# Feature attention of a decoder's third layer: per-token head products on VectorE and GpSimd, or head rounds on rotated rows with sums on TensorE

## Chip, cores and metric
The kernel runs on one core of a Trainium2 chip. The metric is the device time of one execution in microseconds (us), the median of three runs. The core has five engines with queues of their own: TensorE (PE; its weight loads are shown as PEld), VectorE (DVE), ScalarE (ACT), GpSimd (POOL) and SyncE (SP), which here issues transfers (DMA).

## The reference, cut to the stage that changes
The program is a four-layer decoder in float32 over 4 sequences of 256 tokens with 256 features: twelve stages (attention, cross attention or state space, feed forward, per layer), each of the form x = x + f(layernorm(x)). The change lies in the seventh, the third layer's attention. It has 16 query heads and 8 key and value heads of 16 features each; key head h // 2 serves query head h.

```python
q = rope(h @ Wq.T + bq); k = rope(h @ Wk.T + bk); v = h @ Wv.T + bv      # per head, 16 features
def feats(x, R):
    x = x / max(sqrt(sum(x * x)), 1e-6)
    p = einsum('...d,ed->...e', x, R)                                    # R is 8 x 16
    return concatenate([sin(p), cos(p)], -1) / sqrt(16)
qp, kp = feats(q, R), feats(repeat(k, 2), R)                             # b h s f
kv  = einsum('bhsf,bhsd->bsfd', kp, repeat(v, 2))                        # summed over the heads h
out = einsum('bhsf,bsfd->bhsd', qp, kv)
out = out.reshape(b, s, 256)          # heads before tokens, not transposed back
return out @ Wo.T + bo
```

There is no sum over tokens: for each token the output of query head h is the sum over the 8 key heads k of (qp[h] . kp[k]) * v[k], times 2. The `reshape` mixes heads and tokens, so the result has to be stored by heads and read back as rows.

## The kernel before
T = 1024 tokens, P = 128 partitions, KD = 2 chunks of 128 features, TILES = 8 tiles of 128 tokens, HALF = 512. PSUM is used as four "pairs" of 1024 float32 columns (`m.pair(0)` to `m.pair(3)`). `Jobs` hands the pairs out in turn: a named job is filled by PE and emptied by the engine named with it, and a job waits until the one four places before it has been emptied. Stages follow one another through the residual `m.resid`; the next stage begins when this one's last addition to it is done.

`feature_attention` runs in this order:
- The layer norm (`norm_vector`, `norm_gpsimd`, `norm_tensor`, `norm_scalar`) leaves the turned rows in `m.hT`, features on partitions.
- PE projects q0, q1 and k0 with features on partitions (`project`, L239), each twice, the second time with the halves of a head exchanged; DVE rotates them (`rotate`, L1556 and L1559) and squares them (L2229). Then PE makes v with tokens on partitions (L2173), and DVE adds its bias (L2231).
- PE sums the squares of each head (L2182); ACT takes the root (L2207), DVE inverts it. PE multiplies by the random matrix (L2189), which also puts tokens on partitions; DVE scales and reduces the angles (L2247 to L2252); ACT takes the sine (L2211).
- The body: for each of 8 tiles of 128 tokens `head_products` makes all 8 x 8 x 16 products of a query chunk with the keys, a reduction sums over the 16 features (L2267), a second `head_products` multiplies weights with values, and a reduction sums over the 8 key heads (L2259). The products of query chunk 0 are made on DVE, those of chunk 1 on GpSimd; all reductions are DVE's. PE does nothing here. SP stores each finished tile by heads to `l2a_scratch` (L2139).
- The end: SP loads the four sequences back as rows (L2143); PE turns them (L2196), ACT copies them to `m.hT` (L2215), PE projects with Wo (`project_tokens`, L252), DVE adds the bias (L261) and the result (L267).

A float32 matmul is two PE instructions in the trace's counts; a PE transpose is one.

Of the kernel before, what the change touches and what calls it, by code (L numbers as in the profile page):

```python
# [20 lines left out]
ALU = mybir.AluOpType  # L21
# [2067 lines left out]
def feature_attention(m, n, j):  # L2089

    nc = m.nc
    tag = "l2a_"
    w = lambda name: m.w[tag + name]
    HPC, HD = 8, 16
    chunks = [("q", 0), ("q", 1), ("k", 0)]
    jobs = Jobs(m, tag + "in", 2, [(f"{x}{c}{s}", "vector") for x, c in chunks for s in ("", "s")]
                + [("v", "vector"), ("norm", "scalar")] + [(f"p{x}{c}", "vector") for x, c in chunks]
                + [("t0", "scalar"), ("t1", "scalar"), ("out0", "vector"), ("out1", "vector")])  # L2100
    tmp = [m.sb(tag + f"rot{i}", [P, B, S]) for i in range(2)]
    x = {f"{k}{c}": m.sb(tag + f"{k}{c}", [P, T]) for k, c in chunks}
    sq = {f"{k}{c}": m.sb(tag + f"sq_{k}{c}", [P, T]) for k, c in chunks}
    feats = {"q0": m.pair(1), "q1": sq["q1"][:], "k0": sq["k0"][:]}
    v = m.sb(tag + "v", [P, TILES, P])
# [4 lines left out]
    weight = [m.pair(3)[:, 0:HPC * HPC].rearrange("p (k q) -> p k q", q=HPC), m.sb(tag + "weight1", [P, HPC, HPC])[:]]  # L2110
    att = m.sb(tag + "att", [P, TILES, D])
    (rotated, turns_ready, feats_ready, v_ready, pair_done, weight_done, value_done, att_done) = (
        m.sem(tag + s) for s in ("rotated", "turns", "feats", "v_ready", "pair", "weight", "value", "att"))

    def head_products(eng, ops, c, t, step, done):


        if step == 0:
            q = feats[f"q{c}"][:, t * P:(t + 1) * P].rearrange("p (h f) -> p h f", f=HD)
            k = feats["k0"][:, t * P:(t + 1) * P].rearrange("p (h f) -> p h f", f=HD)  # L2120
            ops.tensor_tensor(pair_prod[c][:], q.unsqueeze(1).to_broadcast([P, HPC, HPC, HD]),
                              k.unsqueeze(2).to_broadcast([P, HPC, HPC, HD]), ALU.mult).then_inc(done, 1)
        else:
            g = weight[c].rearrange("p k q -> p q k").unsqueeze(2).to_broadcast([P, HPC, HD, HPC])
            vt = v[:, t, :].rearrange("p (k d) -> p d k", d=HD).unsqueeze(1).to_broadcast([P, HPC, HD, HPC])
            ops.tensor_tensor(value_prod[c][:], g, vt, ALU.mult).then_inc(done, 1)
# [5 lines left out]
    with nc.Block(name=tag + "block", no_gpsimd_drain=True) as block:  # L2132
# [13 lines left out]
        def _(pool):  # L2146
# [5 lines left out]
            for t in range(TILES):  # L2152
# [4 lines left out]
                if t:  # L2157
                    pool.wait_ge(att_done, 2 * t)
# [847 lines left out]
```

## Time and profile before

| | |
|---|---|
| median of 3 runs | 1628.77 us (1625.76 to 1629.52) |
| time of the profiled execution | 1629.11 us |
| its span, first to last instruction | 1627.3 us |
| mean granted TensorE clock | 0.843 of full |
| the stage (first norm instruction to last addition) | 870.63 to 1011.33 us |
| of it the body (products and reductions) | 925.3 to 989.1 us |
| of it the end (store, load, turn, project, add) | 989.1 to 1011.3 us |

The span is 1.8 us shorter than the execution's own time; the difference lies outside the instructions. "PEclk" in the rows is the clock granted to TensorE: 1.00 is 2.4 GHz and 0.50 is 1.2 GHz. In the views by window, the columns are the window, its length, the busy time and number of instructions of each engine, the granted clock, the mean busy share of the 16 DMA engines, and what they moved.

### The profile page before, as it was taken

How to read it: one execution, taken by the hardware profiler on the slowest of the kernel's cores; microseconds unless marked ns; L12 is line 12 of the kernel's file. 1: busy time of each engine (PE TensorE's matmuls, PEld its weight loads, DVE VectorE, ACT ScalarE, POOL GpSimd, SP SyncE). 2: the span in 40 equal slices, each digit the busy share in tenths (PEclk: the TensorE clock that was granted, in tenths of full speed). 3: DMA queues.
4: the chain of work that ended last, by engine and by line, in shares of the span. 5: the costliest groups of instructions: out<-in, count | busy, mean ns of one | idle time of the engine just before them, and what ended most of it. 6: DMA issues, size and time to landing. Idle time of an engine off the chain costs nothing. (4 is left out here: it accounts for less than half of the span.)

```text
span 1627.3 us, 20923 instructions
## 1 busy us (share of the span) xinstructions
PE 1088.7 (67%) x5866; PEld 694.1 (43%) x5866; DVE 1082.2 (67%) x1807; ACT 486.5 (30%) x943; POOL 600.8 (37%) x604
## 2 busy tenths in 40 slices
PE   7545548999218795555998503699847878866970
PEld 3211135776015672113565402577534324445860
DVE  6999975873686548998885795320345868845454
ACT  3423322333402342332221100333313346632430
POOL 0046614552754115661000272023431632214746
PEclk9669977999559897997998756899878969986995
DMA  5064347995321404435100011142520040038944
GB/s 188 30 258 150 108 156 225 313 309 207 98 61 46 112 3 156 154 104 208 41 1 0 0 16 36 47 140 81 164 87 10 26 131 3 3 116 238 340 143 121
DMA packets 135201, 188.51 MB, mean 116 GB/s; under 512 B 34736, under 2 KB 98242, under 8 KB 133836
## 3 DMA queue, kind: packets, MB, share of 16 engines
q1 hardware_dynamic: 100956, 138.51, 26.9%
q0 software_dynamic: 12704, 29.36, 6.2%
q10 hardware_dynamic: 21456, 19.60, 3.8%
q8 instruction: 42, 0.69, 0.2%
q14 instruction: 43, 0.35, 0.1%
HBM read 142.80 MB, written 31.72 MB: 107 GB/s over the span
## 5 line engine op out<-in xcount | busy, mean ns | idle before, releaser
L165 POOL TENSOR_SCALAR rstd<-moments 128x4 f32<-128x4 f32 x24 | 6.5, 269 | 406.0 <-DVE moments L148 406.0
L177 PE MATMUL psum<-w_ident,h 128*128 128x128 f32 x144 | 29.6, 388 | 112.1 <-DVE h L155 112.1
L558 PE MATMUL psum<-l0s_read,w_ident 128*128 128x512 f32 x128 | 65.2, 634 | 52.6 <-DVE l0s_read L623 52.6
L558 PE MATMUL psum<-l1s_read,w_ident 128*128 128x512 f32 x128 | 65.3, 636 | 52.3 <-DVE l1s_read L623 52.3
L1906 DVE TENSOR_REDUCE l3x_neg<-psum 128x2 f32<-128x512 f32 x128 | 80.7, 684 | 23.2 <-PE psum L1777 23.2
L546 POOL TENSOR_TENSOR l1s_drive<-l1s_du,l1s_bc 128x1024 f32<-128x1024 f32 x32 | 75.3, 2353 | 35.3 <-DVE psum L619 35.3
L546 POOL TENSOR_TENSOR l0s_drive<-l0s_du,l0s_bc 128x1024 f32<-128x1024 f32 x32 | 75.3, 2353 | 35.3 <-DVE psum L619 35.3
L1881 ACT ACTIVATE l3x_work<-psum 128x512 f32<-128x512 f32 x128 | 72.7, 599 | 50.9 <-PE psum L1800 50.6
L1028 POOL DMA_INDIRECT l0f_x<-l0f_h_rows,l0f_token_now x56 | 60.4, 1078 | 50.3 <-PE psum L1152 23.7
L1162 PE MATMUL psum<-l0f_w_in,l0f_xT 128*128 (+1 forms) x224 | 77.9, 472 | 0.1
L1037 POOL DMA_INDIRECT l3f_x<-l3f_h_rows,l3f_token_of x64 | 59.3, 926 | 49.1 <-DVE l3f_token_of L1433 28.6
L177 PEld LDWEIGHTS psum<-w_ident,h 128*128 128x128 f32 x144 | 25.3, 201 | 118.5 <-DVE h L155 116.2
L619 DVE TENSOR_TENSOR_SCAN psum<-psum,l0s_drive 128x1024 f32<-128x1024 f32 x32 | 73.2, 2286 | 0.0
L619 DVE TENSOR_TENSOR_SCAN psum<-psum,l1s_drive 128x1024 f32<-128x1024 f32 x32 | 73.2, 2286 | 0.0
L189 ACT ACTIVATE hT<-psum 128x512 f32<-128x512 f32 x36 | 19.4, 596 | 163.8 <-PE psum L177 163.7
L558 PEld LDWEIGHTS psum<-l0s_read,w_ident 128*128 128x128 f32 x128 | 22.4, 195 | 95.3 <-DVE l0s_read L623 79.5
L558 PEld LDWEIGHTS psum<-l1s_read,w_ident 128*128 128x128 f32 x128 | 22.4, 195 | 95.2 <-DVE l1s_read L623 79.2
L595 ACT ACTIVATE psum<-late,w_l1s_a 128x1024 f32<-128x1024 f32 x32 | 35.7, 1118 | 80.0 <-DVE l1s_read L623 79.4
L595 ACT ACTIVATE psum<-l0s_delta,w_l0s_a 128x1024 f32<-128x1024 f32 x32 | 35.7, 1117 | 80.0 <-DVE l0s_read L623 79.4
L1181 PE MATMUL psum<-l0f_w_down,l0f_gatedT 88*128 (+1 forms) x224 | 57.6, 380 | 0.0
L1192 PE MATMUL psum<-l3f_xT,l3f_w_in 128*96 128x96 f32 x528 | 57.0, 252 | 0.5 <-ACT l3f_xT L1293 0.5
L2196 PE MATMUL psum<-w_ident,h 128*128 128x128 f32 x16 | 3.7, 425 | 79.3 <-DMA h<-l2a_scratch 79.3
(635 smaller groups left out, 3145.5 us busy)
## 6 DMA issues: line engine op xcount, KB each, us to landing
l0f_w_in<-in_l0f_w_in SPq DMA_DIRECT2D x56, 352.0 KB
l0s_bc<-l0s_scratch SPq DMA_DIRECT2D x16, 1024.0 KB, 5.2
l1s_bc<-l1s_scratch SPq DMA_DIRECT2D x16, 1024.0 KB, 5.1
l3f_w_in<-in_l3f_w_in SPq DMA_DIRECT2D x32, 384.0 KB
l0f_w_down<-in_l0f_w_down SPq DMA_DIRECT2D x56, 176.0 KB
l2f_w_in<-in_l2f_w_in SPq DMA_DIRECT2D x24, 352.0 KB
l0f_y_rows<-l0f_y ACTq DMA_DIRECT2D x56, 128.0 KB
l3f_w_down<-in_l3f_w_down SPq DMA_DIRECT2D x32, 192.0 KB
```

Of the source, the lines that this page charges most:

```text
L177: ins = nc.tensor.transpose(m.psum[:, at:at + P], m.h[:, t, k * P:(k + 1) * P], m.ident[:])
L546: nc.gpsimd.tensor_tensor(drive[c], du[:, c, :], bc[s][:, 0, :], ALU.mult).then_inc(drive_ready, 1)
L558: ins = nc.tensor.matmul(m.pair(2 + c)[:, cols], lhsT=m.ident[:], rhs=rhs[:, cols], start=start, stop=stop, skip_group_check=True)
L595: nc.scalar.activation(decay[c], delta[:, c, :], ACT.Exp, scale=w["a"][:, c, bass.ds(at, 1)]).then_inc(decay_ready, 1)
L619: nc.vector.tensor_tensor_scan(state[c], decay[c], drive[c], 0.0, ALU.mult, ALU.add).then_inc(scanned, 1)
L1028: nc.gpsimd.indirect_dma_start(x[s][:], None, h_rows, bass.IndirectOffsetOnAxis(ap=token_now[s // 2][:, s % 2:s % 2 + 1], axis=0)).then_in ...
L1037: nc.gpsimd.indirect_dma_start(x[b % ROWS][0:L, :], None, h_rows, bass.IndirectOffsetOnAxis(ap=token_of[0:L, b:b + 1], axis=0)).then_inc(x ...
L1162: ins = nc.tensor.matmul(in_ps[d % 2], lhsT=xT[d % 2][:, k, :], rhs=w, start=(k == 0), stop=(k == KD - 1))
L1181: ins = nc.tensor.matmul(y_ps[d % 2], lhsT=gatedT[d % 2][:, c, :], rhs=w, start=(c == 0), stop=(c == chunks - 1))
L1192: ins = nc.tensor.matmul(feature_ps[i][:, f, :], lhsT=w_in[:, at, k, f * F:(f + 1) * F], rhs=xT[i][:, k, 0:L], start=(k == 0), stop=(k == ...
L1881: nc.scalar.activation(self.prob[i % 8][:, 0:self.keys], self.bank(3 + i % 3)[:, 0:self.keys], ACT.Exp).then_inc(self.exp_done, 1)
L1906: ins = nc.vector.tensor_reduce(self.neg[k % 2][:, :, hl], bank[:, 0:self.keys].rearrange("p (q k) -> p q k", q=self.maxima), AX_X, ALU.ma ...
```

## The change
The body is written anew, and what stands around it follows.
- **Layout.** v is projected with features on partitions too. After the sine, PE turns the features of k0, q0 and q1 back (eight transposes each, new jobs `fk0`, `fq0`, `fq1`), and ACT copies them to rows: the keys to `keys[:, 0, :]`, the queries to `q_rows`. The order of the chunks is now k0, q0, q1. ACT, no longer DVE, adds v's bias, into `values[:, 0, :]`.
- **Rotated copies.** SP makes seven copies of the values and seven of the keys, rotated by 16 r partitions (one head), SBUF to SBUF: two transfers a copy. Values: 14 transfers of 1024 columns. Keys: 14 for each half of the tokens, 28 in all, of 512 columns.
- **Rounds.** For each half of the tokens and each rotation r (16 steps) DVE multiplies both query chunks with the rotated keys (`by_heads`, 1024 elements a partition), PE multiplies by a 128 x 128 matrix of ones within a head, so each feature row holds the head pair's weight (`weigh`, two 512-column matmuls), DVE multiplies that from PSUM with the rotated values (`mix`), and PE adds the product to a running sum in PSUM with the identity (`add`, two 512-column matmuls). PE's order is weigh(s), add(s - 1).
- **Sums.** For each half ACT copies the sums, PE turns them in eight transposes (`turn_sums`; the first half's stand in PE's order at step 10), ACT copies them to `att`, SP stores four tiles and loads two sequences, PE turns eight blocks (`turn_rows`), ACT copies (`take_rows`), PE projects (`project_out`), DVE adds. The bias of the output is added to the residual before the norms' wait, not at the end. GpSimd has only its part of the layer norm.

```diff
+    chunks = [("k", 0), ("q", 0), ("q", 1)]
+    keys, values = (m.sb(tag + s, [P, ROUNDS, T]) for s in ("keys", "values"))
+    turned_to = {"k0": keys[:, 0, :], "q0": q_rows[:, 0, :], "q1": q_rows[:, 1, :]}
+    weights_ps = [m.pair(2 + i).rearrange("p (c t) -> p c t", c=KD) for i in range(2)]
-    pair_prod = [m.sb(tag + f"pair_prod{c}", [P, HPC, HPC, HD]) for c in range(KD)]
-    value_prod = [m.sb(tag + f"value_prod{c}", [P, HPC, HD, HPC]) for c in range(KD)]
+    prod = [m.sb(tag + f"prod{i}", [P, KD, HALF]) for i in range(2)]
+    mixed = [m.sb(tag + f"mixed{i}", [P, KD, HALF]) for i in range(3)]
+    def rotate_heads(sp, rows, r, cols, sem):
+        at = P - HD * r
+        sp.dma_start(rows[0:at, r, cols], rows[HD * r:P, 0, cols]).then_inc(sem, 16)
+        sp.dma_start(rows[at:P, r, cols], rows[0:HD * r, 0, cols]).then_inc(sem, 16)
...
         def _(sp):
+            sp.wait_ge(jobs.empty("v"), 1)
+            for r in range(1, ROUNDS):
+                rotate_heads(sp, values, r, slice(0, T), values_in)
+            sp.wait_ge(jobs.empty("fk0"), 3)
+            for h in range(2):
+                for r in range(1, ROUNDS):
+                    if h:
+                        sp.wait_ge(keys_in[r], 32)
+                    rotate_heads(sp, keys, r, halves[h], keys_in[r])
+            for h in range(2):
+                sp.wait_ge(att_done, h + 1)
+                for t in range(4 * h, 4 * h + 4):
+                    dst = scratch[t // 2, :, t % 2 * P:(t % 2 + 1) * P, :].rearrange("h s d -> s h d")
+                    sp.dma_start(dst, att[:, t, :].rearrange("p (h d) -> p h d", d=HD)).then_inc(stored[t // 2], 16)
+                for b in range(2 * h, 2 * h + 2):
+                    sp.wait_ge(stored[b], 32)
+                    sp.dma_start(m.h[:, 2 * b:2 * b + 2, :], rows[b]).then_inc(att_back[h], 16)
...
         def _(pool):
             norm_gpsimd(m, pool, n)
-            head_products(pool, nc.gpsimd, 1, 0, 0, pool_pair)
-            for t in range(TILES):
...
...
         def _(pe):
-            jobs.wait_room(pe, "v")
-            for t in range(TILES):
-                for k in range(KD):
...
+            project(m, pe, jobs, "v", wcols(w("v"), 0), hT, KD)
+            def weigh(s):
+                pe.wait_ge(prod_done, s + 1)
+                if s >= 2:
+                    pe.wait_ge(mix_done, s - 1)
+                for c in range(KD):
+                    ins = nc.tensor.matmul(weights_ps[s % 2][:, c, :], lhsT=w("same")[:], rhs=prod[s % 2][:, c, :], start=True,
+                                           stop=True)
+            def add(s):
+                h, r = divmod(s, ROUNDS)
+                pe.wait_ge(mix_done, s + 1)
+                for c in range(KD):
+                    ins = nc.tensor.matmul(m.pair(h)[:, c * HALF:(c + 1) * HALF], lhsT=m.ident[:], rhs=mixed[s % 3][:, c, :],
+                                           start=(r == 0), stop=(r == ROUNDS - 1), skip_group_check=True)
+            for s in range(STEPS):
+                weigh(s)
+                if s:
+                    add(s - 1)
+                if s == ROUNDS + 2:
+                    turn_sums(0)
+            add(STEPS - 1)
+            turn_rows(0)
+            turn_sums(1)
+            project_out(0)
+            turn_rows(1)
+            project_out(1)
...
         def _(act):
+            nc.scalar.activation(values[:, 0, :], jobs.pair("v"), ACT.Identity, bias=w("v_b")[:, 0:1])
             for i, (k, c) in enumerate(chunks):
                 act.wait_ge(turns_ready, i + 1)
+                nc.scalar.activation(sq[f"{k}{c}"][:], sq[f"{k}{c}"][:], ACT.Sin, scale=SIN_SCALE).then_inc(feats_ready, 1)
+                jobs.wait_filled(act, f"f{k}{c}")
+                nc.scalar.activation(turned_to[f"{k}{c}"], jobs.pair(f"f{k}{c}"), ACT.Copy)
+            take_sums(0)
+            take_sums(1)
+            take_rows(0)
+            take_rows(1)
...
         def _(dve):
+            o.link(dve, nc.vector.tensor_tensor(m.resid[:], m.resid[:], w("o_b")[:].unsqueeze(1).to_broadcast([P, TILES, D]),
+                                                ALU.add))
+            dve.wait_ge(jobs.empty("norm"), 2)
...
-            for t in range(TILES):
-                head_products(dve, nc.vector, 0, t, 0, pair_done)
...
-            add_tokens(m, dve, jobs, ("out0", "out1"), bias=w("o_b")[:])
+            def by_heads(s):
+                if r:
+                    dve.wait_ge(keys_in[r], 32 * (h + 1))
+                nc.vector.tensor_tensor(prod[s % 2][:], q_rows[:, :, halves[h]],
+                                        keys[:, r, halves[h]].unsqueeze(1).to_broadcast([P, KD, HALF]), ALU.mult).then_inc(prod_done, 1)
+            def mix(s):
+                dve.wait_ge(weighed, s + 1)
+                if s == 1:
+                    dve.wait_ge(values_in, 32 * (ROUNDS - 1))
+                nc.vector.tensor_tensor(mixed[s % 3][:], weights_ps[s % 2],
+                                        values[:, r, halves[h]].unsqueeze(1).to_broadcast([P, KD, HALF]), ALU.mult).then_inc(mix_done, 1)
+            by_heads(0)
+            for s in range(STEPS):
+                if s + 1 < STEPS:
+                    by_heads(s + 1)
+                mix(s)
```

## Rows read from the trace of the kernel before
**Rows 1.** The page: busy time of each engine over the span.
```profile
span 1627.3 us, 20923 instructions
PE 1088.7 (67%) x5866; PEld 694.1 (43%) x5866; DVE 1082.2 (67%) x1807; ACT 486.5 (30%) x943; POOL 600.8 (37%) x604
```
**Rows 2.** Windows of the stage: before the body, and the body.
```profile
890.00:925.00 35.00, 26.61 (x150) 21.40 (x148) 22.83 (x24) 4.52 (x5) 0.00 (x0) 0.83 0.00 0
925.00:989.00 64.00, 0.00 (x0) 0.00 (x0) 61.11 (x49) 0.23 (x1) 49.81 (x16) 0.50 0.13 14
```
**Rows 3.** Timeline: start, duration, engine, line, operation, idle time before and releaser.
```profile
922.92 1.23 DVE L2252 TENSOR_TENSOR l2a_sq_k<-l2a_sq_k,l2a_whole 128x1024 f32<-128x1024 f32 x1
924.17 1.06 ACT L2211 ACTIVATE l2a_sq_k<-l2a_sq_k 128x1024 f32<-128x1024 f32 x1 [2.65 <-DVE l2a_sq_k L2252]
...
925.33 1.23 DVE L2121 TENSOR_TENSOR l2a_pair_prod<-psum,l2a_sq_k 128x1024 f32<-128x1024 f32 x1 [1.19 <-ACT l2a_sq_k L2211]
...
987.85 1.22 DVE L2259 TENSOR_REDUCE l2a_att<-l2a_value_prod 128x128 f32<-128x1024 f32 x1 [1.05 <-POOL l2a_value_prod L2126]
...
995.89 3.67 PE L2196 MATMUL psum<-w_ident,h 128*128 128x128 f32 x16 [79.29 <-DMA h<-l2a_scratch]
...
1000.68 9.38 PE L252 MATMUL psum<-w_l2a_o,hT 128*128 128x256 f32 x32 [1.11 <-ACT hT L2215]
1006.72 1.23 DVE L267 SCALAR_TENSOR_TENSOR resid<-psum,resid 128x1024 f32<-128x1024 f32 x1 [15.45 <-PE psum L252]
1010.10 1.23 DVE L267 SCALAR_TENSOR_TENSOR resid<-psum,resid 128x1024 f32<-128x1024 f32 x1 [2.15 <-PE psum L252]
```
**Rows 4.** Groups by line and form, from the stage (busy, mean ns; idle and releaser).
```profile
L239 PE MATMUL psum<-hT,w_l2a_k 128*128 128x512 f32 x16 | 7.0, 593 | 0.0
L2173 PE MATMUL psum<-w_l2a_v,hT 128*128 128x128 f32 x32 | 3.7, 275 | 0.0
L2247 DVE TENSOR_TENSOR l2a_sq_q<-psum,l2a_norm 128x1024 f32<-128x1024 f32 x2 | 2.5, 1225 | 1.4 <-PE psum L2189 1.4
L2215 ACT ACTIVATE hT<-psum 128x1024 f32<-128x1024 f32 x2 | 2.0, 1024 | 73.4 <-PE psum L2196 73.4
L2621 PE MATMUL psum<-w_ident,l1f_inner 128*128 128x128 f32 x8 | 1.1, 280 | 1.9 <-DVE l1f_inner L2466 1.9
```
**Rows 5.** Windows that show the granted clock and what PE did.
```profile
820.00:840.00 20.00, 20.00 (x69) 11.67 (x69) 17.09 (x20) 3.07 (x3) 0.00 (x0) 1.00 0.00 1
913.00:916.60 3.60, 3.60 (x32) 3.42 (x31) 3.45 (x4) 0.00 (x0) 0.00 (x0) 1.00 0.00 0
919.50:920.00 0.50, 0.00 (x0) 0.00 (x0) 0.50 (x1) 0.00 (x0) 0.00 (x0) 0.84 0.00 0
1000.50:1005.00 4.50, 4.32 (x10) 3.51 (x11) 0.00 (x0) 0.13 (x1) 0.00 (x0) 0.50 0.00 0
1005.00:1005.50 0.50, 0.50 (x3) 0.39 (x3) 0.00 (x0) 0.00 (x0) 0.00 (x0) 0.83 0.00 0
```
**Rows 6.** Transfers by tile: issue time min/median/max, starts; time to landing min/median/max.
```profile
L2139 SPq DMA_DIRECT2D l2a_scratch<-l2a_att x8: 359/360/389, 937.7 to 989.1; - x8
DMA to landing us min/median/max: 2.9/3.0/3.0
...
L2143 SPq DMA_DIRECT2D h<-l2a_scratch x4: 360/469/940, 989.5 to 992.2; - x4
DMA to landing us min/median/max: 3.2/3.5/4.0
...
L1694 SPq DMA_DIRECT2D l1a_q_packed<-l1a_parts x36: 532/599/767, 496.5 to 552.6; - x36
```
**Rows 7.** Windows: one 128 KB store of the body; SBUF-to-SBUF copies of the second layer.
```profile
938.50:939.00 0.50, 0.00 (x0) 0.00 (x0) 0.50 (x1) 0.00 (x0) 0.50 (x2) 0.50 0.65 67
939.00:939.50 0.50, 0.00 (x0) 0.00 (x0) 0.47 (x2) 0.00 (x0) 0.50 (x1) 0.50 0.92 112
939.50:940.00 0.50, 0.00 (x0) 0.00 (x0) 0.50 (x1) 0.00 (x0) 0.50 (x1) 0.50 0.74 83
...
505.00:510.00 5.00, 5.00 (x13) 2.21 (x12) 3.32 (x3) 0.53 (x1) 1.79 (x1) 1.00 0.26 67
```

More of the change, by code:

```diff
@@ L2111, in feature_attention @@
+    summed = m.sb(tag + "summed", [P, KD, HALF])
     att = m.sb(tag + "att", [P, TILES, D])
[L2112 to L2126, printed above, removed]
@@ new lines, in add, with turn_sums @@
+            def add(s):
[4 more added lines that the diff above has]
+                                           start=(r == 0), stop=(r == ROUNDS - 1), skip_group_check=True)
+                ins.then_inc(added, 1)
+            def turn_sums(h):
+                pe.wait_ge(sums_taken, h + 1)
+                for t in range(4):
+                    for c in range(KD):
+                        ins = nc.tensor.transpose(m.pair(h)[:, t * D + c * P:t * D + (c + 1) * P], summed[:, c, t * P:(t + 1) * P],
+                                                  m.ident[:])
+                ins.then_inc(sums_turned, 1)
@@ new lines, in turn_rows, with project_out @@
+            def turn_rows(h):
+                pe.wait_ge(att_done, h + 1)
+                pe.wait_ge(att_back[h], 32)
+                for c in range(KD):
+                    for t in range(4):
+                        ins = nc.tensor.transpose(m.pair(h)[:, c * HALF + t * P:c * HALF + (t + 1) * P],
+                                                  m.h[:, 4 * h + t, c * P:(c + 1) * P], m.ident[:])
+                ins.then_inc(rows_turned, 1)
+            def project_out(h):
+                pe.wait_ge(hT_done, h + 1)
+                for t in range(4):
+                    for k in range(KD):
+                        ins = nc.tensor.matmul(m.pair(2 + h)[:, t * D:(t + 1) * D], lhsT=m.hT[:, k, (4 * h + t) * P:(4 * h + t + 1) * P],
+                                               rhs=w("o")[:, k, :], start=(k == 0), stop=(k == KD - 1))
+                ins.then_inc(out_filled, 1)
@@ L2205, in _ @@
             norm_scalar(m, act, j)
+            m.wait_weights(act, tag)
+            jobs.wait_filled(act, "v")
+            nc.scalar.activation(values[:, 0, :], jobs.pair("v"), ACT.Identity, bias=w("v_b")[:, 0:1]).then_inc(jobs.empty("v"), 1)
             jobs.wait_filled(act, "norm")
@@ L2279, in context_mixing @@
+            by_heads(0)
[3 more added lines that the diff above has]
+                mix(s)
+            for h in range(2):
+                dve.wait_ge(out_filled, h + 1)
+                r = m.resid[:, 4 * h:4 * h + 4, :]
+                nc.vector.tensor_tensor(r, m.pair(2 + h).rearrange("p (t d) -> p t d", d=D), r, ALU.add).then_inc(out_added, 1)
+            dve.wait_ge(out_added, 2)
 def context_mixing(m, n, j):
@@ L2946, in layouts @@
     d["l2a_v"] = rows_to_chunks(i["L2_attn_Wv"].T)
-    d["l2a_v_b"] = across(i["L2_attn_bv"])
+    d["l2a_v_b"] = column(i["L2_attn_bv"])
     d["l2a_o"] = rows_to_chunks(i["L2_attn_Wo"].T)
```

113 lines of the change are left out of this document (45 added, 68 removed).

## The prediction
> **What bounds the kernel now.** The page comes first: over the span PE and DVE are busy alike, 67% each, so the average names no engine [rows 1]. Then the windows of the stage: in the body DVE is busy 61.1 of 64 us, GpSimd 49.8, and PE not at all, at a granted clock of 0.50; transfers take 13% [rows 2]. So the body is DVE's. The timeline gives its ends: the first product starts at 925.33, the last reduction ends at 989.07, 63.7 us [rows 3]. The stage's end, from there to the last addition at 1011.33, is 22.3 us, and it is a chain with nothing beside it: store, load, 16 transposes from 995.89, copies, 16 matmuls from 1000.68, two additions [rows 3]. The next stage needs the last of them, so a microsecond taken from or put on this chain is one of the kernel's time.
>
> **Before the body.** PE sets this stretch (busy 26.6 of its 35 us, without a gap until the last random product) [rows 2]. v as four 512-column float32 matmuls costs 4 x 0.86 = 3.44 us, from the k0 projection (eight such matmuls, 7.0 us: 0.87 with its edge, 0.43 us an instruction), where it cost 3.7 [rows 4]. I take 0.3 us off all that follows. v's bias on ACT and the output bias (2.3 us of DVE) fall into waits: ACT has nothing to do there, and DVE waits for the norms. Without that cover they would cost 1.0 and 2.3 us.
>
> The last angles are ready at 924.15 in the kernel before [rows 3], so at 923.85. ACT then needs a sine (1.06 us, [rows 3]), PE eight transposes, ACT a copy of 1024 columns (1.02, [rows 4]). Transposes: 16 took 3.67 us at clock 0.50, so 1.84 for eight [rows 3]; at the start of another burst eight took 1.1 us [rows 4]. I take 1.84 for q0's and q1's: the clock fell to 0.50 within 919.5 to 920.0, some 3 us after PE's last work at 916.6 [rows 5]. The three chains queue on ACT: k0's copy ends by about 920.4, q0's at 924.35, q1's at 928.35. The first product starts there instead of at 925.33: **+3.0 us**.
>
> **The sixteen steps.** For DVE a step is two operations of 1024 elements, one of them reading PSUM: 2 x 1.225 = 2.45 us [rows 4]. For PE it is four 512-column matmuls: 4 x 0.86 = 3.44 us at full clock. PE is the longer. Do the waits hold it up? mix(s) needs weigh(s); PE meanwhile does add(s - 1) and weigh(s + 1), 3.44 us, before it needs mix(s), which takes 1.2. by_heads runs a step ahead. So no. The sum: 16 x 3.44 = 55.0 us; the first product before PE can begin, 1.2; the first half's eight transposes inside the steps, 1.1. To this comes the clock. In the end of the kernel before, matmuls started at 1000.68 at clock 0.50 and got full clock in the window from 1005.0 to 1005.5 (mean 0.83) [rows 5], so about 4.4 us at half speed, which loses 2.2. Once up it stays: a stretch of 20 us with PE always busy shows 1.00 [rows 5]. Together 59.5 us: the steps end at 928.35 + 59.5 = 987.9, where the old body ended at 989.07: **-4.2 us** against its 63.7. Bounds: no half-clock start, -2.2; 0.05 us more at each of the 32 handovers (the gap from ACT's last copy to the matmuls at 1000.68 is about that), +1.6.
>
> So 111 us of DVE and POOL work (61.1 and 49.8) become 55 of PE, and the gain is small because DVE and POOL had worked side by side.
>
> **The transfers that must come first.** Values: 7 copies x 128 rows x 4 KB = 3.67 MB from 903.4, after ACT's v; then keys, 7 x 0.26 MB for the first half, from 920.4. SP issues an SBUF-to-SBUF copy in 0.6 us [rows 6]: 14 take 8.4 us. The nearest rate is that of the second layer's SBUF-to-SBUF copies: 67 GB/s at a DMA share of 0.26, 258 GB/s at full share [rows 7]. The values then take 14.2 us, to 918.6, and keys round 1 lands some 3 us after 920.4; it is needed at about 931.8, since weigh(0) ends at 933.0. Later rounds come each 1.2 us and are used each 3.44. Hidden, cost 0. SP has issued everything by 937, long before the first half's stores, and that half's store and load (at about 963 to 975) lie under the steps.
>
> **The end.** From the end of the steps: copy 1.02, eight transposes 1.1 (turn_rows(0) ran during the copy), copy 1.02, with handovers 3.35 us. Then four stores at once. One store occupies all DMA engines for (0.65 + 0.92 + 0.74) x 0.5 = 1.15 us [rows 7] and lands after 3.0 [rows 6], so about 1.85 of latency. Four: 4 x 1.15 + 1.85 = 6.4 us. The second load waits for them and lands 3.2 later (3.2 to 4.0, [rows 6]): 9.6. Then eight transposes 1.84, copy 1.03, eight matmuls 6.0 (the old first half: 1000.68 to its addition at 1006.72, [rows 3]), an addition 1.23, handovers 0.2. The clock is low again, since project_out(0) is over 5 us before. Sum 3.35 + 9.6 + 10.3 = 23.25 against 22.3: **+1.0 us**. Half the turning and projecting has gone under the waits (with project_out(0) as cover); the turning of the sums and three more stores in a burst take it back. Bounds: stores that do not queue, -2.3; matmuls at full clock, -2.6; each store only after the one before has landed (4 x 3.0) and a load of 4.0, +6.4.
>
> **Sum.** +3.0 - 4.2 + 1.0 = -0.2 us. The profiled execution took 1629.11, 0.3 above the median of 1628.77; on it this gives 1628.9, on the median **1628.6 us**. A measurement of this kernel can tell about 0.2%, 3.3 us, from no change.
>
> **Rivals.**
> *A, the clock stays up (faster).* If the transposes before the steps, and those after the load, keep or bring the clock, then the steps lose no 2.2, q1's and the last rows' transposes cost 1.1 (-1.5), the last matmuls 3.4 instead of 6.0 (-2.6): -6.3, 1622.3 us. For it: the clock was still 1.00 for 3 us after PE stopped. Against: in the old end 3.67 us of transposes and 4.5 of matmuls went by at 0.50 [rows 3, 5]. 0.17.
>
> *B, the rotated copies are late (slower).* The slowest rate in the rows is the store's, 131 KB in 1.15 us, 114 GB/s, with runs of 64 bytes [rows 7]. At it, values and keys round 1 (3.93 MB) need 34.5 us from 904.4 and land at 939.7, 7.9 us after 931.8: 1636.5 us. It costs something below 148 GB/s, and more than 0.2% below 131. Against: the copied runs are of 2 and 4 KB. 0.11. The Trainium skill (DMA: Bandwidth & Descriptors, section Bandwidth) says to batch transfers to 1 MiB and more, and gives 138 GB/s for one of 64 KB; by an estimate from that page 3.93 MB take 28.5 us and the kernel is 1.9 us slower, at 1630.5. No row here shows that for transfers queued behind one another.
>
> *C, the last burst (slower).* Four stores and two loads one after another by their landings, as bounded above: +6.4, 1635.0 us. For it: nothing hides them now. Against: stores and loads did overlap before, four loads landing within 6.4 us of the first's issue [rows 3, 6]. It leaves 0.2% from 3.5 us on. 0.13.
>
> *D, PE at half clock through the steps.* 64 x 0.86 more, less the 2.2 counted: +52.8, 1681.4. Rows of long busy stretches speak against it. 0.03.
>
> **Chances.** The forecast has 0.56: of it 0.48 within 0.2%, 0.03 faster, 0.05 slower. With A 0.20 faster; with B, C and D 0.32 slower; 0.48 same. The range runs from A to B, 1622.3 to 1636.5, and leaves out D and the tails. The forecast's own range is 1625 to 1632.
>
> **What the profile of the changed kernel would show.** Steps: PE busy without gaps, a 512-column instruction each 0.43 us, granted clock 1.00 from the second step on, DVE busy some 70%; DVE's waits ended by PE. If mix or by_heads waits for a DMA at step 1, it is B. The first by_heads at 928.4, the last add at 987.9, four stores issued from 991.3, the last transposes from 1000.9, the last addition ending at 1011.1. A last-matmul window at 1.00 shows A; transposes after 1004, C. The prediction is wrong outright if PE's steps take other than 3.44 us.

## The result, and the profile after

| | before | after |
|---|---|---|
| median of 20 runs each | 1627.01 us (1622.46 to 1632.67) | 1633.10 us (1624.84 to 1636.79) |
| ratio to before, 95% interval | | 1.0032 (1.0021 to 1.0042) |
| profiled execution: time, span | 1629.11, 1627.3 us | 1632.82, 1631.0 us |
| mean granted TensorE clock | 0.843 | 0.867 |
| the stage, first norm instruction to the next stage's | 141.52 us | 141.01 us |

By the ratio the changed kernel is slower by 0.32%, 5.2 us (3.4 to 6.8); the two medians are 6.1 us apart, the two profiled executions 3.7. In these two profiles the stage that was changed is not longer. Its parts first: the page, the windows from the last projections to the end of the steps (891.20 to 932.20, then 932.20 to 991.20, with 940 to 985 out of their middle), and the end.

```profile
span 1631.0 us, 21259 instructions
PE 1150.4 (71%) x6010; PEld 720.5 (44%) x6010; DVE 1057.6 (65%) x1790; ACT 494.3 (30%) x951; POOL 550.3 (34%) x588
```
```profile
891.20:932.20 41.00, 33.12 (x156) 23.78 (x154) 26.44 (x26) 10.25 (x10) 0.00 (x0) 0.85 0.46 125
932.20:991.20 59.00, 57.62 (x138) 26.06 (x139) 37.71 (x32) 2.05 (x2) 0.00 (x0) 0.96 0.28 57
940.00:985.00 45.00, 45.00 (x112) 20.37 (x111) 30.68 (x27) 2.05 (x2) 0.00 (x0) 1.00 0.25 38
991.20:1015.00 23.80, 13.11 (x56) 10.23 (x54) 2.45 (x2) 3.98 (x4) 0.00 (x0) 0.78 0.36 44
```
The body was DVE's [rows 2] and is now PE's: 45.00 us busy of 45. DVE has become the one that waits, as the groups of the steps show (busy, mean ns, then idle and releaser): 19.1 us for the sums of `weigh`.
```profile
L2198 PE MATMUL psum<-l2a_prod,w_l2a_same 128*128 128x512 f32 x64 | 31.5, 620 | 2.5 <-DVE l2a_prod L2323 2.5
L2206 PE MATMUL psum<-l2a_mixed,w_ident 128*128 128x512 f32 x64 | 29.9, 592 | 0.0
L2333 DVE TENSOR_TENSOR l2a_mixed<-psum,l2a_values 128x1024 f32<-128x1024 f32 x16 | 19.6, 1224 | 19.1 <-PE psum L2198 19.1
```
The timeline of the changed kernel, with the points that answer to [rows 3]:
```profile
907.52 0.60 SPq L2129 DMA_DIRECT2D l2a_values<-l2a_values  x1
...
923.84 0.51 SPq L2129 DMA_DIRECT2D l2a_keys<-l2a_keys  x1
...
932.21 2.36 DVE L2323 TENSOR_TENSOR l2a_prod<-l2a_q_rows,l2a_keys 128x1024 f32<-128x1024 f32 x2 [4.34 <-ACT l2a_q_rows L2263]
...
933.58 5.23 PE L2198 MATMUL psum<-l2a_prod,w_l2a_same 128*128 128x512 f32 x8 [2.53 <-DVE l2a_prod L2323]
...
987.60 3.60 PE L2206 MATMUL psum<-l2a_mixed,w_ident 128*128 128x512 f32 x8
...
994.49 4.12 SPq L2150 DMA_DIRECT2D l2a_scratch<-l2a_att  x4
...
999.43 3.30 SPq L2153 DMA_DIRECT2D h<-l2a_scratch  x2
1005.16 1.94 PE L2223 MATMUL psum<-w_ident,h 128*128 128x128 f32 x8 [6.01 <-DMA h<-l2a_scratch]
1007.14 1.02 ACT L2274 ACTIVATE hT<-psum 128x1024 f32<-128x1024 f32 x1 [11.77 <-PE psum L2223]
1008.22 5.49 PE L2231 MATMUL psum<-w_l2a_o,hT 128*128 128x256 f32 x16 [1.11 <-ACT hT L2274]
1013.74 1.22 DVE L2345 TENSOR_TENSOR resid<-psum,resid 128x1024 f32<-128x1024 f32 x1 [13.33 <-PE psum L2231]
1016.00 0.43 DVE L145 BATCH_NORM_STATS2 stats<-resid 128x6 f32<-128x256 f32 x1 [1.03 <-PEq L2925]
```
Read against the stage's own start (874.99; 870.63 before): the first product comes at 57.22 us instead of 54.70 (+2.5), the steps last 59.0 instead of 63.74 (-4.7), and from there to the last addition's end it is 23.8 instead of 22.3 (+1.5). Together -0.7, and -0.5 at the next stage's first instruction.

So the time came from elsewhere. Cut at the first norm instruction of each stage (the DVE rows of L145), the profiles of three executions of either program say where:

| stage, us | before: shown, r1, r4 | after: shown, r2, r3 |
|---|---|---|
| third layer's attention (changed) | 141.5, 140.7, 140.7 | 141.0, 143.4, 140.8 |
| the three stages after it, summed | 251.4, 248.0, 248.1 | 247.9, 251.3, 250.5 |
| last attention (l3x) | 185.1, 184.3, 184.1 | 185.4, 186.4, 186.2 |
| last stage, routed experts (l3f), to the end | 178.65, 178.61, 178.57 | 181.62, 181.67, 181.58 |

The three stages summed have a spread of their own (one of them, the third layer's experts, takes 174 or 176 us in either program); so have the stages ahead of the change (experts of the first layer 254.2 to 257.3). The last attention goes with that spread: it is about 1 us longer where the third layer's experts took 176 us. Like compared with like it is 1.2 us longer in the changed kernel: 185.4 against 184.3 and 184.1 beside 174 us, 186.4 and 186.2 against 185.1 beside 176. The changed stage has a spread too: r2's 143.4 us differ from the 141.0 shown above mostly by slower matmuls at the start of the steps (6.62 us for the first eight instructions of `weigh` against 5.23) and in the last projection (6.18 us against 5.49). The last stage has no such spread: +3.0 us, and its instructions are the same. Its start in both kernels, PE and the first norm instruction:
```profile
1448.65 1.40 DVE L145 BATCH_NORM_STATS2 stats<-resid 128x6 f32<-128x256 f32 x4 [0.84 <-PEq L2853]
1452.29 3.63 PE L177 MATMUL psum<-w_ident,h 128*128 128x128 f32 x16 [5.74 <-DVE h L155]
1455.75 3.68 PE L1090 MATMUL psum<-w_l3f_router,hT 128*128 128x64 f32 x32
```
```profile
1449.38 1.41 DVE L145 BATCH_NORM_STATS2 stats<-resid 128x6 f32<-128x256 f32 x4 [1.14 <-PEq L2925]
1453.02 3.68 PE L177 MATMUL psum<-w_ident,h 128*128 128x128 f32 x16 [6.04 <-DVE h L155]
1456.49 6.93 PE L1090 MATMUL psum<-w_l3f_router,hT 128*128 128x64 f32 x32
```
The router's 32 matmuls take 6.93 us instead of 3.68. The windows say why: the last column but two is the granted clock, 0.99 over the router's matmuls before and 0.50 after, 1.2 instead of 2.4 GHz. The first two rows of each block are windows of 2 us from the stage's start on.
```profile
1448.65:1450.65 2.00, 0.00 (x0) 0.00 (x0) 2.00 (x10) 0.00 (x0) 0.22 (x1) 0.56 0.28 51
1450.65:1452.65 2.00, 0.36 (x2) 0.33 (x3) 2.00 (x11) 0.00 (x0) 1.62 (x4) 0.50 1.08 363
1455.65:1460.65 5.00, 3.78 (x34) 3.64 (x32) 1.78 (x11) 1.08 (x2) 0.00 (x0) 0.99 1.08 276
```
```profile
1449.38:1451.38 2.00, 0.00 (x0) 0.00 (x0) 2.00 (x10) 0.00 (x0) 0.22 (x1) 1.00 0.39 73
1451.38:1453.38 2.00, 0.36 (x2) 0.33 (x3) 2.00 (x10) 0.00 (x0) 1.62 (x4) 0.69 0.91 276
1456.38:1461.38 5.00, 5.00 (x26) 5.00 (x24) 0.63 (x6) 1.09 (x2) 0.00 (x0) 0.50 1.09 294
```
At the stage's start the order is the other way round (0.56 and 0.50 before, 1.00 and 0.69 after): in the kernel before the clock fell earlier in PE's pause and was back over the router's matmuls, in the changed one it fell later and stayed down through them.

### The profile page after: what moved, and what is told of

It reads as the page before. It is cut to its first block and busy times, and to the rows that moved or that the text cites. A ratio compares the mean times of both kernels' runs of the same rounds, so it can differ in the third digit from the quotient of the medians.

```text
span 1631.0 us, 21259 instructions
## 1 busy us (share of the span) xinstructions
PE 1150.4 (71%) x6010; PEld 720.5 (44%) x6010; DVE 1057.6 (65%) x1790; ACT 494.3 (30%) x951; POOL 550.3 (34%) x588
## 5 line engine op out<-in xcount | busy, mean ns | idle before, releaser
L177 PE MATMUL psum<-w_ident,h 128*128 128x128 f32 x144 | 29.7, 388 | 112.4 <-DVE h L155 112.4
L1906 DVE TENSOR_REDUCE l3x_neg<-psum 128x2 f32<-128x512 f32 x128 | 80.6, 683 | 23.1 <-PE psum L1777 23.1
L558 PEld LDWEIGHTS psum<-l0s_read,w_ident 128*128 128x128 f32 x128 | 22.3, 194 | 95.5 <-DVE l0s_read L623 79.6
L1777 PE MATMUL psum<-l3x_k_packed,l3x_q_packed 64*128 64x256 bf16 x256 | 43.9, 307 | 12.8 <-ACTq L2031 8.7
```

The source lines that it names most:

```text
L177: ins = nc.tensor.transpose(m.psum[:, at:at + P], m.h[:, t, k * P:(k + 1) * P], m.ident[:])
L558: ins = nc.tensor.matmul(m.pair(2 + c)[:, cols], lhsT=m.ident[:], rhs=rhs[:, cols], start=start, stop=stop, skip_group_check=True)
L1906: ins = nc.vector.tensor_reduce(self.neg[k % 2][:, :, hl], bank[:, 0:self.keys].rearrange("p (q k) -> p q k", q=self.maxima), AX_X, ALU.ma ...
```

## The experiments

Each ratio is to the kernel before on the same chip, with its 95% interval. Increments ("pads") are of semaphores that nothing waits for, put where the engine idles; they change no result. In the compiled kernel before, PE's stream holds 10930 instructions, ACT's 1620, DVE's 2433, GpSimd's 1058, SP's 1005; in the changed one 11236, 1629, 2436, 1034, 1047. All code behind the stage is therefore moved. "Position" below means where in its engine's stream an instruction stands.

**r1, r2: both programs again.** No edit.

> The kernel before once more, unchanged, as the measure of spread. All theories: ratio 1.000 within its interval. In its profile the attention stage (first norm statistic to the next stage's) takes 141.5 us as in the first profile. If the stages that load expert weights differ by 2 to 3 us from the first profile of the same program, then the 3.0 us by which the first expert stage was longer in the changed kernel's profile (254.2 against 257.3 us) is spread between executions and no effect of the change.

> The changed kernel once more, unchanged. Theory 1 (the loss lies inside the stage, in most executions): the stage takes 145 us or more in this profile, against 141.0 in the first. Theory 2 (the loss lies outside the stage, in stages whose instructions are the same): the stage again takes 141 us, the ratio is again 1.002 to 1.004, and the stages before it are some 3 to 5 us longer than in the kernel before. Theory 3 (spread alone): ratio within 0.1% of 1.

Measured 0.9990 (0.9970 to 1.0009) and 1.0031 (1.0011 to 1.0052). The loss repeats. The first experts stage takes 256.6 us in r1 and 255.5 in r2, so its 3 us between the two profiles shown are spread. The stages ahead of the change are not longer in r2 than in r1 (865.6 and 866.1 us together), and the changed stage took 143.4 us, not the 141 expected.

**r3, r4: the inputs' sizes.** The change also alters two small inputs (`v_b`, `ones`/`same`). r3 gives the changed kernel the old sizes, r4 the old kernel the new ones.

```diff
# r3, on the changed kernel: the old sizes; the ones-within-a-head matrix stands in v_b's place, v's bias in that of ones
-rhs=w("same")[:, 0:P:HD] ... lhsT=w("same")[:] ... bias=w("v_b")[:, 0:1]
+rhs=w("v_b")[:, 0:P:HD] ... lhsT=w("v_b")[:] ... bias=w("ones")[:, 0:1]
-("l2a_v_b", [P, 1]) ... ("l2a_same", [P, P])
+("l2a_v_b", [P, P]) ... ("l2a_ones", [P, 8])
# r4, on the kernel before: inputs in DRAM of the new sizes
+                if name == "l2a_v_b":
+                    src = src.partition_broadcast(P)
+                elif name == "l2a_ones":
+                    src = src[:, 0:8]
```

> The changed kernel with the two small inputs of the stage kept at the sizes of the kernel before (64 KB and 4 KB instead of 512 bytes and 64 KB: the ones matrix travels in the place of the value bias and the other way round), so that every input lies in memory as before. If the difference comes from where the inputs lie in memory (a form of theory 2), the ratio falls from 1.003 to 1.000 within 0.1%. If it comes from the stage (theory 1) or from anything else in the new code, it stays at 1.003.

> The kernel before with the two small inputs at the changed kernel's sizes (512 bytes and 64 KB), its code otherwise the same; the bias is spread over the partitions by its transfer. Placement theory: ratio 1.003. Theory 1 and any theory of the new code: 1.000 within 0.1%.

r4: 0.9987 (0.9970 to 1.0004): new inputs don't slow the old kernel. r3: 1.0016 (0.9997 to 1.0035), by itself undecided; its last two stages are the changed kernel's (186.2, 181.6 us). So it is not the inputs.

**r5, r6, r7: the old kernel with the new stream lengths.**

```diff
# r7; r5 has only PE's, r6 all but PE's
+            for _ in range(306):
+                pe.sem_inc(idle[0], 1)       # before pe.wait_ge(att_back, 16 * B)
+            for _ in range(9): act.sem_inc(idle[1], 1)
+            for _ in range(3): dve.sem_inc(idle[2], 1)
+            for _ in range(42): sp.sem_inc(idle[3], 1)
+            for _ in range(232): pool.sem_inc(idle[4], 1)
```

> The kernel before, computing the same; only PE's instruction stream is made 306 instructions longer in the attention stage, by increments of an unused semaphore while PE waits for the loaded rows, so that all later PE code stands where the changed kernel has it. Position theory (the loss comes from where later code stands, and with it the moments at which PE's clock falls and rises): the last attention takes about 185.5 to 186.4 us instead of 184.1 to 185.1, the last expert stage 181.6 instead of 178.6, the ratio is 1.002 to 1.004; if PE's position is what counts. Any theory in which the new work itself carries the loss: both stages as in the kernel before, ratio 1.000.

> The same with the other four streams made longer instead (ACT 9, DVE 3, SP 42, POOL 232 instructions, while they idle; POOL's code is 24 shorter in the changed kernel, and 232 is 256 less 24), PE's left alone. Position theory with another engine's stream: 181.6 us in the last stage here and 178.6 with PE's. New-work theory: nothing moves.

> The kernel before with all five streams made longer. Position theory, whatever the engine: last attention 185.4 or more, last expert stage 181.6, ratio 1.002 to 1.004. New-work theory: 184.5 and 178.6, ratio 1.000.

r5 1.0017 (1.0002 to 1.0033), r6 1.0018 (1.0001 to 1.0035), r7 1.0032 (1.0013 to 1.0051). r7 computes the stage in the old way, takes 141.65 us for it, and loses what the changed kernel loses; its last two stages are 186.2 and 181.2 us. In r5 and r6 the last stage is 178.4 and 178.8 and the router is at 3.7 us: neither PE's stream alone nor the other four alone brings that loss, though either raises the time a little. The router's row of r7 is the changed kernel's:
```profile
1454.10 3.67 PE L177 MATMUL psum<-w_ident,h 128*128 128x128 f32 x16 [6.03 <-DVE h L155]
1457.56 6.93 PE L1090 MATMUL psum<-w_l3f_router,hT 128*128 128x64 f32 x32
```

**r8, r9, r10: other positions.** r8 lengthens GpSimd's stream of the changed kernel to the old length; r9 puts all five streams of the changed kernel where the old ones stood, modulo 256 instructions; r10 adds 256 to four streams of the old kernel (without DVE).

```diff
# r8, on the changed kernel, after GpSimd's norm
+            for _ in range(24): pool.sem_inc(idle[0], 1)
# r9, on the changed kernel: PE 208 (40 before each q chunk's transposes, 40 before the steps, 88 before turn_rows(1)),
#     ACT 247, DVE 253 (before the last addition), SP 214, GpSimd 24
# r10, on the kernel before, at r7's places: PE, ACT, SP, GpSimd 256 each
```

> The changed kernel with 24 increments of an unused semaphore added to POOL, which has nothing to do there, so that POOL's later code stands where the kernel before has it. If POOL's position counts: last expert stage 178.6 us and ratio 1.001; otherwise 181.6 and 1.003 as in the changed kernel.

> The changed kernel, computing the same, with increments of unused semaphores put where the engines idle (PE 208, ACT 247, DVE 253, SP 214, POOL 24), so that every stream's later code is longer than in the kernel before by 512, 256, 256, 256 and 0 instructions. If what counts is the position within blocks of 256 instructions: last expert stage 178.6 us, last attention 184 to 185, ratio 1.000 within 0.1% (the attention stage itself as before or up to 1 us longer, where the increments do not all fit into idle time). If position counts in another way, any ratio from 1.000 to 1.005. New-work theory: 181.6 and 1.003 again.

> The kernel before with 256 increments each on PE, ACT, SP and POOL in idle time. Position within blocks of 256: nothing moves, last expert stage 178.6 us, ratio 1.000. Absolute position, or idle-time increments costing by themselves: ratio 1.002 to 1.003, as with the other padded kernels.

r8 1.0049 (1.0034 to 1.0063), last stage 181.4: GpSimd's position alone takes nothing back, and the time is above either figure expected. r10 0.9994 (0.9974 to 1.0013), last stage 178.5: length alone costs nothing. r9 1.0113 (1.0084 to 1.0141): the later stages came back near the old values (184.4 and 180.0, the router at 3.7 us), but the pads overran the pauses they were put in, and the stage took 157.8 us.

**r11, r12: fewer sums on PE.** The steps are bound by PE, and GpSimd is free. In r11 GpSimd adds the products of two rounds, and PE sums half as often. r12 is r11 with its code brought to the old positions (PE 14, ACT 247, DVE 254, SP 214, GpSimd 10).

```diff
+            for q in range(ROUNDS):
+                pool.wait_ge(mix_done, 2 * q + 2)
+                if q >= 2:
+                    pool.wait_ge(added, q - 1)
+                nc.gpsimd.tensor_tensor(paired[q % 2], mixed[2 * q % 4], mixed[(2 * q + 1) % 4], ALU.add).then_inc(pair_done, 1)
...
-            def add(s):
-                pe.wait_ge(mix_done, s + 1)
+            def add(q):
+                pe.wait_ge(pair_done, q + 1)
...
-                if s:
-                    add(s - 1)
+                if s % 2 and s > 1:
+                    add(s // 2 - 1)
```

> The changed kernel with half of TensorE's additions taken off it: POOL adds the products of each two rounds, and PE adds eight such sums instead of sixteen products. Tests that the steps are PE's: PE has 13.8 us less to do there (16 matmul pairs of 0.86 us), DVE's 16 x 2.45 = 39.2 us then stand close to PE's 41.3. Theory of the prediction: the stage takes 129 to 131 us instead of 141. Were the steps bound by DVE or by handovers, the stage would stay within 2 us of 141. Ratio 0.994 to 0.998, since its later code stands at yet another place, which moves the rest by up to 0.3% either way.

> The same with increments in idle time (PE 14, ACT 247, DVE 254, SP 214, POOL 10), so that all later code stands at the kernel before's position within blocks of 256. With that form of the position theory: last expert stage 178.6 us and ratio 0.993. Otherwise 0.993 to 0.998, no better than without the increments.

r11 0.9963 (0.9944 to 0.9982): faster than both kernels; stage 133.6 us, last stage 178.9. The steps were PE's, but the 129 to 131 us expected were missed by 3 us (see r18). r12 1.0021 (1.0004 to 1.0039), not 0.993: later stages 184.3 and 179.4, but the stage took 145.6 us, since DVE's pads held up the last addition, as its row shows (the matmuls that it needs had ended at 1004.0):
```profile
1014.86 1.23 DVE L2366 TENSOR_TENSOR resid<-psum,resid 128x1024 f32<-128x1024 f32 x1 [23.09 <-issue]
```

**r13 to r16: is it the clock?** Up to here the last stage was 181.2 us or more in five profiles (after, r2, r3, r7, r8), and those are the five in which the router's matmuls took 6.93 us; in the nine others they took 3.7 to 3.9 us and the stage 178.4 to 180.0. To tell cause from company, r13 (old kernel), r14 (changed) and r15 (pair sums) keep PE at work over the boundary. The 16 products also move PE's code behind them, by 64 instructions; no run tells the one from the other. r16 restores the positions of PE, ACT, SP and GpSimd, without pads on DVE.

```diff
# r13, r14, r15: 16 products, overwritten afterwards, at the start of the last stage
             norm_tensor(m, pe, n)
+            if tag == "l3f_":        # stands before the line above
+                for _ in range(16):
+                    nc.tensor.matmul(m.pair(3)[:, 0:P], lhsT=m.ident[:], rhs=m.ident[:], start=True, stop=True)
# r16, on the changed kernel: PE 208 (60 before the norm, 37 before each q chunk's transposes, 37 on either side of
#     project_out(0)), ACT 247, SP 214, GpSimd 24
```

> The kernel before, with 16 extra products of 128 columns on TensorE (the identity with itself, result overwritten) at the start of the last stage, before its norm's transposes; nothing else changed. Theory (the last stage's length hangs on when the clock falls around its start): here the router's 32 matmuls were already at full clock (3.68 us), so at most the transposes gain, whose end the norm sets; last stage 177.0 to 178.6 us, time 0 to 1.6 us lower. Rival (the extra products have a price of their own, or the stage's length has nothing to do with the clock): last stage 178.6 us or more.

> The changed kernel with the same 16 products at the same place. Theory: PE then has no pause of 6 us before the last stage's transposes, the clock does not fall to half in front of the router's matmuls, which take 3.7 us instead of 6.93; last stage 178 to 179 us instead of 181.6, time 3 us below the changed kernel, so 1.001 of the kernel before. Rival (the code's position alone makes the last stage longer, the slow matmuls are a part of what it does there): the last stage stays above 180.5 us and the ratio at 1.003.

> The version in which GpSimd sums pairs of rounds, with the 16 products at the start of the last stage. Its last stage was 178.9 us with the matmuls already at 3.8 us. Theory: like the kernel before with the products, 0 to 1.6 us below 1624; stage of the change 133.6 us as it was. Rival: no gain, 0.996 of the kernel before.

> The changed kernel, lengthened so that the code after the stage stands within its 256-instruction blocks where it stood in the kernel before on PE, ACT, SP and GpSimd (208, 247, 214 and 24 increments of unused semaphores), with PE's put in five pauses and none on DVE, whose position differs by 3. Position theory: last attention 184.4, last stage 178.5 to 180 us, as in the other realigned runs (184.36 and 179.96), and the stage itself 141 to 142: 1.000 to 1.001 of the kernel before. Rival (any lengthening costs, whatever position it gives): last stage over 181 us and 1.003 or more. PE's increments overrun their pauses if one costs over 0.1 us: then the stage is longer, by what its windows show.

r14's timeline, PE at the boundary, and the windows up to the router and over it:
```profile
1450.97 3.81 PE L1086 MATMUL psum<-w_ident 128*128 128x128 f32 x32 [2.40 <-PEq L2928]
1454.62 1.40 PE L177 MATMUL psum<-w_ident,h 128*128 128x128 f32 x8
...
1457.52 3.68 PE L1093 MATMUL psum<-w_l3f_router,hT 128*128 128x64 f32 x32
```
```profile
1450.97:1457.52 6.55, 6.29 (x49) 5.31 (x50) 6.26 (x27) 1.08 (x2) 2.64 (x4) 1.00 0.86 240
1457.52:1461.20 3.68, 3.68 (x34) 3.54 (x32) 1.07 (x8) 1.09 (x2) 0.00 (x0) 1.00 1.10 269
```
The clock stays at 1.00, the router takes 3.68 us, and the last stage is 177.6 us, 4.0 shorter than in the changed kernel and 1.0 shorter than in the old one. By time r14 is 1.0018 (1.0002 to 1.0034) where the changed kernel was 1.0031: the direction is that of the theory, but the intervals overlap. r13: 1.0002 (0.9986 to 1.0017), last stage 178.7: no gain, just outside the theory's 177.0 to 178.6 and where the rival had it. r15: 0.9993 (0.9977 to 1.0009), stage 133.2, last stage 179.2. That is no gain either, and by time the pair sums come out 0.3% slower with the products than without them (r11, and r18 below, its interval just touching). Neither theory had that, and no stage of the profile shows it.

r16: last stage 178.5 us with the router at 3.78, the last attention 184.9 (beside 176 us for the third layer's experts, as 185.1 in the kernel before): the position theory again. The whole is 1.0061 (1.0040 to 1.0082), since PE's 60 pads before the norm's transposes were no free ones. The transposes start 9.1 us into the stage instead of 3.6, and the stage takes 148.1 us:
```profile
879.43 3.65 PE L177 MATMUL psum<-w_ident,h 128*128 128x128 f32 x16 [10.47 <-issue]
```

**r17, r18: the two edits crossed, and the pair sums again.** r17 is r7 with the 16 products; r18 is r11 unchanged.

> The kernel before, lengthened as in r7 (306, 9, 3, 42 and 232 increments), with the 16 products at the start of the last stage. Theory: the code's position acts on the last stage through the clock at its start, so the products take the last stage from 181.2 to 177.6 us as they did in the changed kernel (181.6 to 177.6); the last attention stays at 186 us; time 1.001 of the kernel before, where r7 had 1.0032. Rival (position costs the last stage directly): over 180.5 us, 1.003.

> The version with pair sums on GpSimd once more, unchanged. Stage 133.6 us again, since TensorE has 48 instead of 64 products in the rounds of each of its 512-column forms; last stage 178.9. By the profile 7.4 us below the changed kernel: 0.997 of the kernel before (r11: 0.9963). If r11's median was luck: 0.999, as r15 had it.

r17 1.0012 (0.9994 to 1.0031). The expected 177.6 us did not come: the last stage is 180.6, where the rival had it, though the time is where the theory had it. The router's matmuls are at 3.68 and the experts' token lists are written 32.3 us into the stage, as in r14 (36.1 in r7). But the first gathered tokens come later. PE's rows of r14, then of r17, with the windows 25 to 40 us into the stage:
```profile
1489.78 0.90 PE L1189 MATMUL psum<-w_ident,l3f_x 96*128 96x96 f32 x4 [6.52 <-DMA l3f_x<-l3f_h_rows,l3f_token_of]
```
```profile
1490.39 1.28 PE L1189 MATMUL psum<-w_ident,l3f_x 96*128 96x96 f32 x4 [8.41 <-DMA l3f_x<-l3f_h_rows,l3f_token_of]
```
```profile
1475.97:1490.97 15.00, 6.96 (x34) 5.77 (x33) 8.28 (x19) 1.14 (x3) 5.60 (x6) 0.50 0.89 230
```
```profile
1474.71:1489.71 15.00, 5.92 (x29) 5.03 (x27) 8.30 (x19) 0.63 (x1) 5.62 (x6) 0.50 1.08 253
```
In r17 the DMA engines are still full (share 1.08 against 0.89) when the gathers start, PE waits 1.9 us more, and it gets its clock back later: in the window 44 to 48 us into the stage it is 0.61 in r17 as in the changed kernel, and 1.00 in r14 (0.92 before). In order: before, after, r14, r17:
```profile
1492.65:1496.65 4.00, 4.00 (x37) 3.54 (x36) 1.79 (x6) 1.48 (x5) 2.87 (x4) 0.92 0.49 102
```
```profile
1493.38:1497.38 4.00, 4.00 (x26) 3.53 (x25) 1.19 (x4) 0.97 (x4) 3.09 (x4) 0.61 0.29 82
```
```profile
1494.97:1498.97 4.00, 4.00 (x41) 3.61 (x40) 1.88 (x7) 1.73 (x7) 3.08 (x4) 1.00 0.57 127
```
```profile
1493.71:1497.71 4.00, 4.00 (x25) 3.53 (x25) 1.19 (x5) 0.96 (x5) 3.09 (x4) 0.61 0.32 91
```
This window sorts all twenty profiles, which the router's clock doesn't: 0.60 to 0.63 in the six whose last stage took 180.6 us or more (after, r2, r3, r7, r8, r17), 0.85 to 1.00 in the other fourteen (177.6 to 180.0). So what goes with the longer stage is that TensorE gets its clock back later among the first experts; a slow router is one way there and not the only one. Late tokens alone are not enough: in r13 PE waits 7.39 us for them and they come 40.8 us into the stage, as late as r17's 40.7, and yet that window has 0.85:
```profile
1485.27:1489.27 4.00, 4.00 (x34) 3.56 (x33) 1.26 (x4) 1.51 (x6) 3.07 (x4) 0.85 0.37 103
```
One profile can't say whether r17's late clock belongs to that program or to that execution.

r18 0.9956 (0.9934 to 0.9979), 1622.7 us: r11's gain stands. The stage takes 134.2 us. Its steps, from the first product to the last sum, are 51.4 us instead of 59.0:
```profile
934.31:985.71 51.40, 47.31 (x112) 19.72 (x112) 40.08 (x32) 2.05 (x2) 25.20 (x8) 0.95 0.31 63
```
PE issues 32 instructions of 0.43 us fewer, 13.8 us; 7.6 of it comes out. PE is no longer always busy (47.3 of 51.4). GpSimd's sums and DVE's `by_heads`, which reads two SBUF tiles, hold each other up: the last sum, with `by_heads` over, takes 2.35 us, the seven before it 3.27, and a `by_heads` that starts while a sum is running takes 1.71 us (the first of them 2.25) instead of 1.21 and ends some 1.1 us after the sum. One pair in order:
```profile
948.54 3.26 POOL L2166 TENSOR_TENSOR l2a_sq_q<-l2a_mixed,l2a_sq_k 128x1024 f32<-128x1024 f32 x1 [2.30 <-DVE l2a_sq_k L2342]
...
951.18 1.71 DVE L2332 TENSOR_TENSOR l2a_prod<-l2a_q_rows,l2a_keys 128x1024 f32<-128x1024 f32 x1
```

## Why the prediction was wrong

The forecast was no measurable change, 1628.6; it is 0.32% slower. The sum of the stage was right: -0.2 us forecast, -0.5 between the two profiles shown, and +0.8 between the means of three profiles each.

- *Start, +3.0:* +2.5. The copy of q1 ended at 932.1, and the first product stood right behind it. The transposes of q0 went by at full clock (1.06 us, not the 1.84 taken), those of q1 did not (1.94).
- *Steps, 59.5 us, -4.2:* 59.0, -4.7. PE's instruction took 0.43 us, the handovers cost nothing, and the clock was back between 935 and 940 (0.83 in that window, then 1.00). The half-clock start was there, and shorter than costed: the first eight instructions took 5.23 us where eight later ones take 3.60, so it cost about 1.6 us of the 2.2.
- *Transfers, 0:* right; rival B did not happen. (Its sum slips by 0.8 us: 34.5 us from 904.4 end at 938.9, not 939.7.) The values went at 265 GB/s with the DMA engines full, and DVE never waited for a copy:
```profile
910.00:920.00 10.00, 10.00 (x64) 10.00 (x64) 4.99 (x7) 1.61 (x2) 0.00 (x0) 0.69 1.00 265
```
  The figure that was weighed beside B (the Trainium skill, DMA: Bandwidth & Descriptors, section Bandwidth), 138 GB/s, is for one transfer of 64 KB. The 14 copies of the values are of 64 to 448 KB and queued one behind another; for them the trace shows about twice that rate, so the 1.9 us worked out from the figure did not come.
- *End, 23.25, +1.0:* 23.8, +1.5. Four stores and the second load cost 10.7 us from the first store's issue to the transposes against 9.6 in the sum; the matmuls took 5.5 against 6.0. Rival C (+6.4) did not happen, nor did A: the last transposes stand at 0.50 again and the last matmuls at 0.67, half clock at first:
```profile
1005.16:1007.10 1.94, 1.94 (x8) 1.54 (x8) 0.00 (x0) 0.00 (x0) 0.00 (x0) 0.50 0.00 0
1008.22:1013.71 5.49, 5.48 (x16) 4.21 (x16) 0.00 (x0) 0.00 (x0) 0.00 (x0) 0.67 0.00 0
```
- *Rival D* did not happen.

The step that failed is the one that turned the stage's sum into the kernel's time: "a microsecond taken from or put on this chain is one of the kernel's time", and then "Sum. +3.0 - 4.2 + 1.0 = -0.2 us" on the median. It takes everything outside the stage as fixed. The change altered not only what the stage does but how many instructions each engine's stream holds, and the stages behind it don't run at a fixed speed: the last one goes with when TensorE's clock falls and comes back at its start. It took 3.0 us more, and the last attention, like compared with like, 1.2 more; the other 1.0 of the 5.2 us is within the spread. No rival of the prediction had a mechanism outside the stage, though its range (to 1636.5) held the result.

What is shown: the old algorithm with the new stream lengths loses as much (r7, 1.0032), so the loss needs none of the new work; other lengths lose nothing (r10, 0.9994); and in r9, r12 and r16, with pads to the old positions modulo 256 (in r16 on all engines but DVE), the last two stages come back to 184.3 to 184.9 and 178.5 to 180.0 us. What is argued: that the clock is the way from the positions to the last stage. In all twenty profiles the last stage's length goes with the clock 44 to 48 us into it, and r14's products take 4.0 us off the changed kernel's last stage; but the same products take only 0.6 us off r7's (181.2 to 180.6 in r17), and by time neither r14 nor r17 is clear of the kernel that it was made from. What was only found together: in r5 and r6 the time is up by 0.17 and 0.18% without a longer last stage in their profiles. What stays open: by what the code's position shifts the moment at which the clock falls; why the last attention is 184.1 to 185.1 us at the old positions and 185.3 to 186.4 at the changed ones; and whether r17's late clock was chance. The Trainium skill (Runtime: NRT & Kernel Launch, section Instruction fetch mechanics) says that streams are refilled in blocks of 256 instructions, at a cost that is mostly hidden. r7 and r10 are in keeping with blocks of that size (+256 costs nothing, r7's amounts do), but no run here shows a refill.

## What to carry to other kernels

A sum for one stage predicts that stage; below half a per cent the kernel's time can also hang on stages nobody touched, as here where a short burst of TensorE follows a pause. Compare the stages' lengths one by one before explaining a small difference by the change, and pad the old kernel to the new length to see what the rewriting costs as such. And when a rewrite makes another engine the bound, look at once for what it can hand back: GpSimd's pair sums took 7.6 us off the steps, and are the version to keep (0.9956 and 0.9963, without the 16 products).

## What the runs showed of the hardware that was not expected

- Position matters at the level of 0.3%: 592 added increments in five streams, all in idle places, made the old kernel 1.0032 of itself (r7); 1024 others made it 0.9994 (r10).
- The same 32 matmuls of 64 columns took 6.93 us in five profiles and 3.7 to 3.9 in the others. In the last stage it was steady for a program: three profiles of the old code and three of the changed one, with either inputs, never mixed. In the first experts stage, ahead of all edits, it was not: one and the same program has its router's 32 matmuls at 3.86 us in one execution and at 6.85 in another (the kernel before, then r1), and that stage's length does not follow it (256.9 us with 3.83 in r11, 256.6 with 6.85 in r18, the same program):
```profile
230.49 3.86 PE L1090 MATMUL psum<-w_l0f_router,hT 128*128 128x16 f32 x32
```
```profile
230.64 6.85 PE L1090 MATMUL psum<-w_l0f_router,hT 128*128 128x16 f32 x32
```
- Increments are not free: 254 on DVE filled 23.1 us (r12), 0.09 us each, and 88 on PE a pause of 10.0 us (r9), at most 0.11 each. 60 on PE ahead of the norm's transposes delayed these by 5.5 us (r16).
- A DVE product of two SBUF tiles and a GpSimd sum of SBUF tiles did not run side by side but one behind the other: the product's mean of 1.40 us in r18 is made of 1.21 and of 1.71 or 2.25, where it started during a sum.
